# A band mask written into the score banks by eight 64x32 matmuls in place of two 64x128 ones

## What is computed

```python
qkv = x @ Wqkv                       # 16 heads of 64
q = l2norm(q) * qs; k = l2norm(k) * ksc
q = q * cos * scale + rotate_half(q) * sin * scale      # k with 1/scale
# windows of 32 positions; the keys are the window's own and the one before
mask = (it < jb) | (it > jb + w) | (jb == -1)
sim = jnp.einsum('bhwie,bhwje->bhwij', bq, bk2) * QK_SCALE
sim = jnp.where(mask, -jnp.finfo(sim.dtype).max, sim)
attn = jax.nn.softmax(sim, -1)
out = jnp.einsum('bhwij,bhwje->bhwie', attn, bv2)
```

## Time and profile before

| | |
|---|---|
| median of 3 runs | 3939.11 us |
| lowest and highest | 3936.31 and 3940.21 us |
| the profiled execution | 3927.86 us |
| its span, first to last instruction | 3926.1 us |
| TensorE busy | 3686.9 us |
| mean granted TensorE clock | 0.988 of full speed |
| instructions | 163,005 |

### The profile page before, as it was taken

How to read it: one execution, slowest core, us unless ns; L and a number is a source line. 1 busy time by engine, 2 the same in 40 slices (tenths; PEclk the granted TensorE clock), 3 DMA queues, 4 the chain that set the end, 5 groups by cost and what they waited for, 6 DMA issues and landing times.

```text
span 3926.1 us, 163005 instructions
## 1 busy us (share of the span) xinstructions
PE 3686.9 (94%) x67712; PEld 2840.2 (72%) x67712; DVE 3008.4 (77%) x5061; ACT 2270.5 (58%) x4270; POOL 2597.5 (66%) x3029
## 2 busy tenths in 40 slices
PE   6999979999999999999999999999999999999998
PEld 3555547777767777668877677777677777778876
DVE  7666658878778788778887788877788887888876
ACT  3555546666546666456666466665466664566662
POOL 4545548777548787368887288775478874678870
PEclk8999989999999999999999999999999999999999
DMA  1000012222212222122222122222122221122220
GB/s 44 4 6 4 6 33 68 55 58 60 58 32 60 57 57 59 41 49 60 61 57 56 30 64 56 60 59 60 32 58 56 60 61 41 48 60 60 60 52 22
DMA packets 136307, 189.03 MB, mean 48 GB/s; under 512 B 38006, under 2 KB 58484, under 8 KB 135412
## 3 DMA queue, kind: packets, MB, share of 16 engines
q1 hardware_dynamic: 135540, 178.23, 17.7%
HBM read 22.67 MB, written 2.10 MB: 6 GB/s over the span
## 4 chain that ended last, share of the span: by engine, by line
PE 76%; issue 4%; POOL 3%; DVE 2%; ACT 0%; DMA 0%; POOLq 0%; SPq 0%; DVEq 0%; ACTq 0%
PE PS L1270 18%; PE PS L1417 10%; PE PS L1256 10%; PE PS L1294 8%; PE PS L1280 8%; PE PS L1257 8%; PE PS L1258 8%; PE PS L1476 2%; PE PS L1411 2%; PE PS L1454 1%; PE PS L1447 1%; POOL t L1182 1%; PE PS L1442 1%; POOL t L1187 1%; DVE m L1803 0%
## 5 line engine op out<-in xcount | busy, mean ns | idle before, releaser
L1182 POOL TENSOR_TENSOR t<-t 128x1024 f32<-128x1024 f32 x384 | 908.3, 2370 | 368.2 <-DVE t L1764 366.9
L1187 POOL TENSOR_TENSOR t<-t,rn 128x1024 f32<-128x1024 f32 x384 | 723.6, 1905 | 29.8 <-POOL rn L150 27.3
L1542 ACT ACTIVATE va<-PS 128x512 f32<-128x512 f32 x384 | 229.8, 598 | 631.9 <-PE PS L1258 631.6
L1763 DVE TENSOR_TENSOR t<-PS,rope 128x512 f32<-128x512 f32 x768 | 523.6, 682 | 27.9 <-ACT sq L1577 26.0
L1256 PE MATMUL PS<-w_hi,xh 128*128 128x512 f32 x1152 | 514.7, 447 | 22.8 <-DVE xl L1063 11.3
L1764 DVE TENSOR_TENSOR t<-PS,rope 128x512 f32<-128x512 f32 x768 | 522.9, 681 | 0.0
L1577 ACT ACTIVATE sq<-PS 128x512 f32<-128x512 f32 x768 | 454.2, 593 | 33.0 <-PE PS L1258 17.4
L1270 PE MATMUL PS<-constants,t 128*128 128x128 f32 x3072 | 443.3, 277 | 19.8 <-POOL t L1187 13.2
L1258 PE MATMUL PS<-w_lo,xh 128*128 128x512 f32 x1152 | 458.4, 398 | 0.0
L1257 PE MATMUL PS<-w_hi,xl 128*128 128x512 f32 x1152 | 458.3, 398 | 0.0
L1770 DVE TENSOR_REDUCE ss<-sq 128x16 f32<-128x1024 f32 x384 | 448.5, 1209 | 0.0
(11 more groups left out here) (167 smaller groups left out, 7697.7 us busy)
## 6 DMA issues: line engine op xcount, KB each, us to landing
vs<-va SPq DMA_DIRECT2D x768, 130.0 KB
vs<-va SPq DMA_DIRECT2D x768, 65.0 KB
t<-in_L_ffn_Wqkv SPq DMA_DIRECT2D x18, 512.0 KB, 4.5
w_out<-in_L_ffn_Wo SPq DMA_DIRECT2D x6, 512.0 KB, 3.9
a_normed<-in_L_attn_x SPq DMA_DIRECT2D x8, 256.0 KB, 6.4
a_xo<-in_L_attn_x SPq DMA_DIRECT2D x8, 256.0 KB, 2.9
out<-total SPq DMA_DIRECT2D x8, 256.0 KB, 3.5
w_raw<-in_L_ffn_W SPq DMA_DIRECT2D x6, 341.0 KB
```

The source lines that it names most:

```text
L1182: pool.tensor_tensor(mine[:, i, :], mine[:, i, :], t2[:, i, :], ALU.add).then_inc(done, 1)
L1187: pool.tensor_tensor(h, h, bc(rn[:, H * i:H * (i + 1)], 2, HB), ALU.mult).then_inc(done, 1)
L1763: dve.tensor_tensor(o1, src, bc(rope[:, 2 * i, t, :], 1, 8), ALU.mult)
```

## The change

Each of the two mask matmuls is cut into four of 32 queries, so that there are eight, with 64x32 tiles of the array as the scores have. The moving operand is the same for the four of a half, all 512 columns of it. A semaphore instruction is put between the wait for the mixed values and the masks. The values computed are the same.

```diff
                     turn_k(1)
                     pe.wait_ge(on_made, at(T, 2, 2, 2))
+                    pe.sem_inc(s_begun, 1)
                     for par in range(2):
                         rows = slice(HB * par, HB * (par + 1))
-                        pe.matmul(PS[:, 2 + par, :], sel_bf[rows, :], bc(mask_q[tile1][rows, :], 1, PAIRS),
-                                  start=True, stop=False, skip_group_check=True)
+                        for w in range(NW):
+                            pe.matmul(PS[W * w:W * (w + 1), 2 + par, :], sel_bf[rows, W * w:W * (w + 1)],
+                                      bc(mask_q[tile1][rows, :], 1, PAIRS), start=True, stop=False, skip_group_check=True)
                     score_half(0)
```

## The result

The changed kernel takes 3954.6 us (median of 4 runs, 3951.9 to 3955.9); the kernel before, run beside it, 3937.7 (3931.2 to 3940.2). The ratio is 1.0051, 95% interval 1.0036 to 1.0065: slower by half a per cent, 17 us, where 3916 and a gain had been forecast. The profiled execution took 3955.9 us, with a span of 3954.1. The trace of before is of an execution that was 10 us under its kernel's median, so the two traces lie 28 us apart where the medians lie 17: where in the program the other 11 fall isn't known, and a difference of a few us in one stretch can be that execution's own.

A forecast was written before the change was run, and what follows sets the result against it. TensorE was taken as the bound, busy 3,687 of 3,926 us. 177 slots x 0.13 us = 23.0 us, so 3904.9 for the profiled execution and, 11.2 us under the median, a forecast of 3916; range 3896 to 3936.

The forecast's parts named there:

- The change of shape: Masks to scores: masks in the scores' tile shape bring the first score at 0.23 us, not 0.32; 0.09 us gained.
- The supply of instructions: Masks to projection: 40 score instructions supplied at 10 ns each give 0.98 us against 1.11, 0.13 us gained per slot.
- 177 slots: Slots counted as gaining: 192 less 6 first, 6 second and about 3 at layers' ends; times 0.13 us is 23.0 us.
- Rivals A and B: Masks to scores: A, no change, 3936 to 3939 (15%); B, bf16 column tiles as slow as f32, 3963 (7%).
- What is added: Per slot, six weight loads, six matmuls and one semaphore, costed at nothing; the semaphore uncovered would be 0.05 to 0.1 us.
- Instruction fetch: TensorE's packet stops in mixing groups: boundaries move but hit as often; nothing taken, 9 us to either side.
- whatever TensorE is spared is gained: Ordinary slots: TensorE is busy 13.91 of 13.94 us, so its savings shorten the slot if no other engine ends last.
- Rival C: Mixing groups: packet boundaries fall into many more; 41 more stops of 0.75 us would undo the gain (4%).

The follow-up runs named there:

- column-cut control: Changed kernel's instruction count and semaphore, but the mask cut by columns into eight wide 64x128 matmuls of 128 columns each; 3966.1 us, ratio 1.0064 to the kernel before.
- place 160: Where a layer's end falls in a 256-instruction packet, kernel before at 0: the changed kernel and three with wide masks, ends 525.0 to 526.6 us.
- nine times: Changed kernel with its eight masks issued nine times instead of once in each layer's first slot; 3934.5 us, ratio 0.9984 to the kernel before.

## Why the prediction was wrong

- **The change of shape: right.** First score 0.23 us after the masks, as forecast.
- **The supply of instructions: right in kind, 0.02 us too high.** Masks to projection 1.00 us, forecast 0.98: in the trace 24 scores start within 0.41 us of the first mask, and the other 40 between 0.41 and 0.85, 11 ns each. The gain is 0.11 us and not 0.13. With 177 slots that is 19 us in place of 23.
- **Rivals A and B: out.** The scores' loads run under the masks, and eight bf16 streams run beside each other (391 ns for one, 0.41 us for eight). The rule cited from the Trainium skill ("TensorE: Matmul & The Clock Gate", Part 3), that a load overlaps running matmuls only for another row group, isn't what the trace shows here either: the scores' loads start at 1892.63, while the masks, on the same 64 rows, are recorded until 1893.01. The same part of the page also allows a load ahead into the background weight buffer, and no run here tells whether that is what happens.
- **What is added: right only because the added semaphore is one.** The experiments show that the semaphore instructions aren't free: 58 ns each when twelve more stand ahead of the masks.
- **Instruction fetch, "I take nothing, with 2 stops per layer to either side: 12 x 0.75 = 9 us": this is the step that failed.** I had averaged over the ordinary slots: the boundaries walk through the 27 of a layer, and there an average is fair (the column-cut control has 2356.5 us in them, 5 more than before). A layer's end isn't walked over: it is met at one place, the same five times, because the loop's code stays where it is. There TensorE's matmuls stop for 2.1 and not 0.2 us at L1294, they are busy 2 to 4 us longer at a lower granted clock, and five ends are 24 us. That is neither 2 stops of 0.75 nor bounded by them.
- **"whatever TensorE is spared is gained": wrong by most of it.** Against the column-cut control, at the same places in the packets, the change spares 0.13 us per slot before the projection, some 20 us in 162 slots, and the ordinary slots are only 1 us shorter (2355.5 for 2356.5). The spared time is there again as stops inside the tile groups: 81.7 + 14.8 us at L1294 and L1280 in the changed kernel, and 12 us less in the control, whose lines are

```profile
PE PS L1294 <- issue: 77.8, 88, 2.8
...
PE PS L1280 <- issue: 7.0, 26, 0.5
```

  A stop ends when its packet has come; a slot that arrives earlier can wait longer. Two slots of the changed kernel and, second fence, two of the control show it: the undisturbed kind, and the seventeenth of the third layer, which is 1.3 us longer with the faster masks.

```profile
1892.60:1906.37 13.77, 13.77 (x332) 1.00 0.24 61
1950.09:1965.64 15.55, 14.13 (x333) 1.00 0.22 55
```

```profile
1898.09:1911.90 13.81, 13.81 (x331) 1.00 0.24 61
1956.25:1970.47 14.22, 14.04 (x332) 1.00 0.23 60
```

  The twenty-third slot is longer with the faster masks in all six layers, by 0.26 to 1.51 us; the seventeenth isn't in two of them. That the faster slot is the cause is argued from these, not shown: it rests on one trace of each, and the stops of one slot differ between layers too. Over whole runs the change is ahead of the control by 12 us in the medians and 5 by the ratios, whose intervals overlap.
- **Rival C was the right mechanism with the wrong place and price.** It asked for 41 more stops in the ordinary slots and got 4%. 11 more stops at L1294 were enough, because five of them last 1.9 us and more, and behind those the granted clock of the layers' ends is lower.

What stays open: whether the lower clock in the ends is the stops' doing (at place 160 the ends have 0.95 to 0.98; nine times, without the long stop at L1294, still has 0.97 to 0.99 where before had 0.98 to 1.00; the two weren't separated), and with it the 14 of the 24 us that are longer matmuls; what spreads the runs of one program by 19 to 29 us; and how the kernel before does with its masks repeated in the first slots, which wasn't tried.

## What to carry to other kernels

Where one engine's stream of instructions is long and comes in bursts, a change of its length is a change of every packet boundary behind it; cost it by listing where the stops are now, above all in code that a loop meets at a fixed place, and take the spread over placements (here 31 us for the kernel before between two places, 23 for the changed one between five) as part of the range. To tell a change's own effect from its placement, build a control with the same number of instructions and the old behaviour, and compare stretch by stretch; read the totals last. Filler is only filler if the sequencer has time for it: repeat work that is hidden, rather than add semaphores.

## What the runs showed of the hardware

- TensorE's instructions came in packets of 256 (16 KB). A stop for one inside a burst of tile matmuls lasted 0.5 to 1.4 us in ordinary slots and up to 2.8 us at a layer's end.
- 128 instructions moved the same kernel by 31 us beyond their own cost (the kernel before, 3985.1 against 3938.0 with 16 us of prelude).
- Semaphore increments on TensorE started 153 ns apart in a row of 128, and the first mask came 118 ns later for each; ahead of the masks one cost nothing and twelve more 58 ns each.
- Eight 64x32 bf16 matmuls of 512 columns together took 0.41 us, where two 64x128 ones took 0.39; without a change of tile shape behind them the next group started 0.09 us sooner.
